# A graph layer's fused kernel: the vectors g and u by VectorE's row sums, u by way of device memory, and the queues ordered anew

## The reference

```python
h = relu(layernorm(x))
q, k, v = h @ Wq + bq, h @ Wk + bk, h @ Wv + bv
adj = zeros(N, N).at[src, dst].set(1)
a = q @ k.T / sqrt(512);  a = a*adj + (1 - adj)*(-1e6)
x = x + softmax(a) @ v
h = relu(layernorm(x))
agg = segment_sum(h[src], dst) / max(deg, 1)
x = x + (h + alpha * (agg @ W.T + b))
```

## Time and profile before

| | |
|---|---|
| median of 3 runs | 240.35 us (240.06 to 240.42) |
| the profiled execution, its own time | 240.38 us |
| its span, first to last instruction | 238.6 us |
| TensorE busy | 232.7 us (98%), 1296 instructions |
| VectorE busy | 163.4 us (68%), 282 |
| ScalarE busy | 80.8 us (34%), 147 |
| GpSimd busy | 71.5 us (30%), 104 |
| granted clock of TensorE | 1.00 in all 40 slices |
| chain that ended last | TensorE 86%, VectorE 10%, DMA 2% |

### The profile page before, as it was taken

The page is one execution under the profiler, slowest core; times in us unless marked ns, Lnnn a source line. Parts: engine busy times, 40 slices in busy tenths (PEclk is TensorE's granted clock), DMA queues, the critical chain, the costliest instruction groups (busy, mean ns, idle before and its releaser), DMA issues.

```text
span 238.6 us, 3313 instructions
## 1 busy us (share of the span) xinstructions
PE 232.7 (98%) x1296; PEld 188.5 (79%) x1296; DVE 163.4 (68%) x282; ACT 80.8 (34%) x147; POOL 71.5 (30%) x104
## 2 busy tenths in 40 slices
PE   7999799999999999999999999999999999999995
PEld 5476489788888888888888888888888888888885
DVE  6999999998979482885749975757574263064222
ACT  3299972843222132233260623232342002060000
POOL 4187172000000019971431643434153306000000
PEclk9999999999999999999999999999999999999999
DMA  6990000000000001040000000000000000001232
GB/s 210 332 371 17 1 3 0 0 3 0 0 3 26 18 3 47 3 140 36 0 0 3 0 0 0 3 0 1 0 0 3 0 0 0 3 3 44 94 122 92
DMA packets 5616, 9.41 MB, mean 39 GB/s; under 512 B 864, under 2 KB 1376, under 8 KB 5600
## 3 DMA queue, kind: packets, MB, share of 16 engines
q1 hardware_dynamic: 4880, 8.91, 10.5%
q10 hardware_dynamic: 720, 0.28, 0.4%
HBM read 7.09 MB, written 2.10 MB: 39 GB/s over the span
## 4 chain that ended last, share of the span: by engine, by line
PE 86%; DVE 10%; DMA 2%; issue 0%; ACTq 0%; DVEq 0%
PE bank L804 22%; PE bank L806 21%; PE bank L805 21%; PE bank L953 12%; PE bank L825 5%; DVE ohW L553 3%; DVE ohL L549 3%; PE bank L973 3%; DMA src_i<-in_src 2%; DVE hT_lo L604 1%; DVE M_lo L634 1%; PE bank L864 1%; PE bank L889 0%; PE bank L851 0%; DVE key_b L540 0%
## 5 line engine op out<-in xcount | busy, mean ns | idle before, releaser
L804 PE MATMUL bank<-V_hi,pT_hi 128*128 128x512 f32 x64 | 25.6, 401 | 0.0
L422 ACT ACTIVATE h2f<-xs,nmr,rstd 128x512 f32<-128x512 f32 x8 | 6.5, 816 | 56.3 <-POOL nmr L365 56.3
L549 DVE TENSOR_TENSOR ohL<-iotaL,lo_b 128x1024 bf16<-128x1024 bf16 x33 | 22.6, 686 | 4.0 <-PE bank L825 4.0
L553 DVE TENSOR_TENSOR ohW<-iotaW,key_b 128x1280 bf16<-128x1280 bf16 (+4 forms) x33 | 25.2, 763 | 0.0
L804 PE MATMUL bank<-hT_hi,GT_hi 128*128 128x512 f32 x64 | 25.1, 392 | 0.0
L806 PE MATMUL bank<-V_hi,pT_lo 128*128 128x512 f32 x64 | 25.0, 391 | 0.0
L806 PE MATMUL bank<-hT_hi,GT_lo 128*128 128x512 f32 x64 | 25.0, 390 | 0.0
L953 PE MATMUL bank<-A,h_hi 128*128 128x512 f32 x64 | 24.9, 389 | 0.0
L953 PE MATMUL bank<-A,h_lo 128*128 128x512 f32 x64 | 24.9, 389 | 0.0
L805 PE MATMUL bank<-hT_lo,GT_hi 128*128 128x512 f32 x64 | 24.9, 389 | 0.0
L805 PE MATMUL bank<-V_lo,pT_hi 128*128 128x512 f32 x64 | 24.9, 389 | 0.0
(11 more groups left out here) (135 smaller groups left out, 528.2 us busy)
## 6 DMA issues: line engine op xcount, KB each, us to landing
xs<-in_x SPq DMA_DIRECT2D x4, 512.0 KB, 9.2
out_dram<-o_sb SPq DMA_DIRECT2D x7, 256.0 KB, 2.0
wq_raw<-in_wqT SPq DMA_DIRECT2D x4, 256.0 KB, 6.4
wk_raw<-in_wkT SPq DMA_DIRECT2D x4, 256.0 KB, 7.1
wv_raw<-in_wv SPq DMA_DIRECT2D x1, 1024.0 KB, 12.7
wt_raw<-in_wT SPq DMA_DIRECT2D x1, 1024.0 KB, 5.4
bv_sb<-in_bv SPq DMA_DIRECT2D x1, 256.0 KB, 3.3
b_sb<-in_b SPq DMA_DIRECT2D x1, 256.0 KB, 3.1
```

The lines of the kernel that those rows point to most:

```text
L422: nc.scalar.activation(out, xs[:, t, :], ACT.Relu, bias=nmr[:, layer, t:t + 1], scale=rstd[:, layer, t:t + 1]).then_inc(relu, 1)
L549: nc.vector.tensor_tensor(ohL[:, q % RING, :, :].rearrange("p b (m two) -> p b m two", two=2), bcast(iotaL[:, :].rearrange("p (m two) -> p ...
L553: nc.vector.tensor_tensor(ohW[:, q % RING, :, 0:row].rearrange("p b (m two) -> p b m two", two=2), bcast(iotaW[:, 0:row].rearrange("p (m t ...
L804: mm(out, lhs[0][a], rhs[0][b], start=(first and k == 0), stop=False)
```

## The change

g and u are no longer summed over partitions by TensorE. wk and wq are loaded a second time, untransposed (`wk_rows`, `wq_rows`, 1 MB each), with bq and bk broadcast to all partitions (256 KB each). VectorE makes each element of g and u by one row sum (four `tensor_tensor_reduce` for each vector, each waiting for the one before). g then stands where it is needed. u stands as four numbers on each partition; SyncE stores it to a line of 2 KB in device memory, waits, and reads it back broadcast to `u_sb`. Steps `g` and `u` of TensorE, VectorE and ScalarE are gone, and there are 20 in place of 21 steps in the rotation of banks. The three orders are written anew and GpSimd has one of its own. The keys are made in fewer VectorE instructions (window numbers are moved by one; the check for edges outside their window becomes two sums on ScalarE, for which `bb` has one more product), the copy `lo_b` goes to ScalarE and the products of biases to GpSimd. The first tile of wk and src change queues. The core of the diff:

```diff
-PE_ORDER = ("Mk0 Mk1 c1 bb c2 M0 c2 T0 c1 M1 T1 c1 T2 c1 M2 c1 M3 c1 T3 c2 G0 T4 G1 G2 g c2 T5 c1 G3 T6 T7 u c3 G4 G5 G6 c3 "
-           "V0 c3 V1 V2 V3 c2 G7 V4 c2 V5 c2 V6 V7 c3")
-ACT_ORDER = ("sum0 sum1 sq0 sum2 sum3 k0 sq1 sq2 rows0 k1 sum4 T0 rows1 sq3 rows2 sum5 T1 T2 k2 sum6 sq4 M0 M1 rows3 M2 M3 "
-           "k3 T3 k4 wv0 rows4 sq5 sum7 sq6 T4 rows5 sq7 k5 G0 T5 rows6 k6 G1 rows7 T6 T7 G2 G3 u G4 k7 wv1 k8 G5 G6 k9 V0 "
-           "k10 V1 V2 k11 V3 G7 k12 k13 V4 V5 V6 k14 V7 k15")
-DVE_ORDER = ("o4 bb o4 T0 o3 T1 T2 M0 o1 M1 M2 M3 T3 gsum o1 usum o2 T4 g wv0 o2 G0 T5 o1 T6 G1 T7 G2 o2 dot0 dot1 G3 dot2 "
-           "wv1 u o2 G4 o2 dot3 G5 dot4 G6 V0 o1 V1 o3 dot5 o1 V2 dot6 V3 G7 o2 V4 dot7 o2 V5 V6 V7")
+PE_ORDER = ("Mk0 Mk1 c3 bb M0 c2 M1 c2 T0 M2 T1 M3 T2 T3 c3 G0 G1 G2 G3 c1 V0 T4 c3 V1 T5 c3 T6 V2 V3 T7 c3 V4 V5 c3 G4 G5 "
+           "G6 c3 V6 c2 G7 c2 V7 c3")
+ACT_ORDER = ("sum0 sum1 sq0 sum2 sq1 sq2 k0 sum3 rows0 M0 k1 sum4 M1 rows1 sq3 T0 rows2 M2 T1 rows3 k2 M3 T2 T3 wv0 k3 wv1 "
+           "sum5 sq4 G0 sq5 rows4 G1 k4 sum6 G2 T4 sq6 rows5 k5 sum7 G3 rows6 k6 T5 sq7 V0 k7 V1 rows7 T6 k8 V2 T7 V3 k9 "
+           "k10 V4 V5 G4 G5 G6 k11 V6 k12 G7 k13 k14 V7 k15")
+DVE_ORDER = ("o7 bb o2 M0 o1 M1 T0 T1 M2 M3 T2 T3 o1 wv0 usum gsum wv1 o1 G0 o2 dot0 G1 dot1 o3 dot2 T4 G2 o1 G3 V0 o1 T5 o1 "
+           "dot3 o1 V1 dot4 o1 T6 o1 V2 T7 V3 dot5 V4 o1 V5 o1 dot6 dot7 o1 G4 G5 G6 o2 V6 o4 G7 o1 V7")
+POOL_ORDER = ("sum0 sum1 sum2 sq0 sq1 sum3 sq2 sum4 sq3 sum5 sq4 sq5 sum6 sq6 sum7 sq7")
...
-        g_terms = place("g_terms", [P, 2, D], F32, r_G + 16 * KB)
-        u_terms = place("u_terms", [P, 2, D], F32, r_V + 24 * KB)
-        t_g, t_u = g_terms[:, 1, :], u_terms[:, 1, :]
+        wk_rows = place("wk_rows", [P, KD, D], F32, r_V + 16 * KB)
+        wq_rows = place("wq_rows", [P, KD, D], F32, r_V + 24 * KB)
+        bq_row, g_scr = (place(n, [P, D], F32, r_G + (16 + 2 * i) * KB) for i, n in enumerate(("bq_row", "g_scr")))
...
+        bk_row = place("bk_row", [P, D], F32, r_R + 6 * KB)
...
-                for raw, w_d, loaded in ((wq_raw, wqT_d, ld_wq), (wk_raw, wkT_d, ld_wk)):
-                    sp.dma_start(raw[:, k, :], w_d[k * P:(k + 1) * P, :]).then_inc(loaded[k], 16)
+                sp.dma_start(wq_raw[:, k, :], wqT_d[k * P:(k + 1) * P, :]).then_inc(ld_wq[k], 16)
+                if k == 0:
+                    sp.dma_start(src_i[:, :], src_d).then_inc(ld_edges, 16)
+                else:
+                    sp.dma_start(wk_raw[:, k, :], wkT_d[k * P:(k + 1) * P, :]).then_inc(ld_wk[k], 16)
             rows_in(2)
             rows_in(3)
             sp.dma_start(wv_raw[:, :, :], wv_d.rearrange("(k p) n -> p k n", p=P)).then_inc(ld_wv, 16)
+            sp.dma_start(wk_rows[:, :, :], wk_d.rearrange("(k p) n -> p k n", p=P)).then_inc(ld_g, 16)
+            sp.dma_start(bq_row[:, :], bqrow_d.partition_broadcast(P)).then_inc(ld_g, 16)
+            sp.wait_ge(strays, 2)
+            sp.dma_start(wq_rows[:, :, :], wq_d.rearrange("(p k) n -> p k n", k=KD)).then_inc(ld_u, 16)
+            sp.dma_start(bk_row[:, :], bkrow_d.partition_broadcast(P)).then_inc(ld_u, 16)
+            sp.wait_ge(u_dots, KD)
+            sp.dma_start(u_d.rearrange("(p k) -> p k", k=KD), u_col[:, :]).then_inc(u_out, 16)
+            sp.wait_ge(u_out, 16)
+            sp.dma_start(u_sb[:, :], u_d.partition_broadcast(P)).then_inc(u_back, 16)
...
-            for step, n in ACT_STEPS:
+            pool.wait_ge(ld_bqk, 32)
+            link(nc.gpsimd.tensor_scalar(bqk_s[:, :, :], bqk[:, :, :], SCALE, None, ALU.mult))
+            nc.gpsimd.tensor_tensor(bprod[:, 0:KD], bqk_s[:, 0, :], bqk[:, 1, :], ALU.mult).then_inc(vec_ready, 1)
+            for step, n in POOL_STEPS:
...
+            act.dma_start(wk_raw[:, 0, :], wkT_d[0:P, :]).then_inc(ld_wk[0], 16)
             act.dma_start(dst_i[:, :], dst_d).then_inc(ld_edges, 16)
-            act.dma_start(src_i[:, :], src_d).then_inc(ld_edges, 16)
...
+            act.wait_ge(src_low, 1)
+            nc.scalar.activation(lo_b[:, :, :], bcast(key_i[0][:, :], 2, 2), ACT.Copy).then_inc(tables, 1)
+            act.wait_ge(past, 1)
+            nc.scalar.activation(stray[:, 0, :], key_t[0][:, :], ACT.Relu, bias=1.0, scale=-1.0,
+                                 accum_out=bprod[:, KD:KD + 1]).then_inc(strays, 1)
+            nc.scalar.activation(stray[:, 1, :], key_t[2][:, :], ACT.Relu,
+                                 accum_out=bprod[:, KD + 1:KD + 2]).then_inc(strays, 1)
...
                 dve.wait_ge(ld_edges, 32)
-                nc.vector.tensor_scalar(key_i[0][:, :], src_i[:, :], P - 1, None, ALU.bitwise_and)
+                nc.vector.tensor_scalar(key_i[0][:, :], src_i[:, :], P - 1, None, ALU.bitwise_and).then_inc(src_low, 1)
                 nc.vector.tensor_scalar(key_i[1][:, :], src_i[:, :], N - P, None, ALU.bitwise_and)
                 link(nc.vector.tensor_tensor(key_t[0][:, :], dst_i[:, :], win0[:, :], ALU.subtract))
-                nc.vector.tensor_copy(lo_b[:, :, :], bcast(key_i[0][:, :], 2, 2))
-                nc.vector.scalar_tensor_tensor(out=key_t[1][:, :], in0=key_i[1][:, :], scalar=1.0 / P, in1=wide[:, :],
-                                               op0=ALU.mult, op1=ALU.mult)
-                link(nc.vector.tensor_tensor(key_t[2][:, :], key_t[0][:, :], wide[:, :], ALU.is_lt))
-                link(nc.vector.scalar_tensor_tensor(out=key_t[3][:, :], in0=key_t[0][:, :], scalar=0.0,
-                                                    in1=key_t[2][:, :], op0=ALU.is_ge, op1=ALU.mult))
-                link(nc.vector.scalar_tensor_tensor(out=key_t[1][:, :], in0=key_t[1][:, :], scalar=1.0, in1=key_t[0][:, :],
-                                                    op0=ALU.add, op1=ALU.add))
-                link(nc.vector.tensor_tensor(key_b[:, :, :], bcast(key_t[1][:, :], 2, 2), bcast(key_t[3][:, :], 2, 2), ALU.mult))
-                nc.vector.tensor_reduce(bprod[:, KD:KD + 1], key_t[3][:, :], AX.X, ALU.min)
-                dve.wait_ge(tables, 2)
+                link(nc.vector.scalar_tensor_tensor(out=key_t[1][:, :], in0=key_i[1][:, :], scalar=1.0 / P, in1=wide[:, :],
+                                                    op0=ALU.mult, op1=ALU.mult))
+                nc.vector.tensor_tensor(key_b[:, :, :], bcast(key_t[1][:, :], 2, 2), bcast(key_t[0][:, :], 2, 2), ALU.add)
+                nc.vector.tensor_tensor(key_t[2][:, :], key_t[0][:, :], wide[:, :], ALU.subtract).then_inc(past, 1)
+                dve.wait_ge(tables, 3)
+                dve.wait_ge(past, 1)
...
-            dve.wait_ge(ld_bqk, 32)
-            link(nc.vector.tensor_scalar(bqk_s[:, :, :], bqk[:, :, :], SCALE, None, ALU.mult))
-            nc.vector.tensor_tensor(bprod[:, 0:KD], bqk_s[:, 0, :], bqk[:, 1, :], ALU.mult).then_inc(vec_ready, 1)
...
-                elif step in ("gsum", "usum"):
-                    weights, raw, terms, done = (0, wk_raw, g_terms, g_sum) if step == "gsum" else (1, wq_raw, u_terms, u_sum)
-                    for k in range(KD):
-                        dve.wait_ge((ld_wk if step == "gsum" else ld_wq)[k], 16)
-                    link(nc.vector.tensor_scalar(terms[:, 0, :], raw[:, 0, :], bqk_s[:, weights, 0:1], None, ALU.mult))
-                    for k in range(1, KD):
-                        ins = nc.vector.scalar_tensor_tensor(
-                            out=terms[:, k % 2, :], in0=raw[:, k, :], scalar=bqk_s[:, weights, k:k + 1],
-                            in1=terms[:, (k - 1) % 2, :], op0=ALU.mult, op1=ALU.add)
-                        if k < KD - 1:
-                            link(ins)
-                    ins.then_inc(done, 1)
+                elif step == "gsum":
+
+                    dve.wait_ge(ld_g, 32)
+                    for m in range(KD):
+                        if m:
+                            dve.wait_ge(g_dots, m)
+                        nc.vector.tensor_tensor_reduce(
+                            out=g_scr[:, :], in0=wk_rows[:, m, :], in1=bq_row[:, :], scale=SCALE, scalar=0.0, op0=ALU.mult,
+                            op1=ALU.add, accum_out=g0[:, m:m + 1]).then_inc(g_kept if m == KD - 1 else g_dots, 1)
+                elif step == "usum":
+
+                    dve.wait_ge(ld_u, 32)
+                    for m in range(KD):
+                        if m:
+                            dve.wait_ge(u_dots, m)
+                        nc.vector.tensor_tensor_reduce(
+                            out=uh[0][:, :], in0=wq_rows[:, m, :], in1=bk_row[:, :], scale=SCALE, scalar=0.0, op0=ALU.mult,
+                            op1=ALU.add, accum_out=u_col[:, m:m + 1]).then_inc(u_dots, 1)
...
-                elif step == "g":
-                    dve.wait_ge(g_ps, 1)
-                    nc.vector.tensor_copy(g0[:, :], bank[7][:, 0:KD]).then_inc(g_kept, 1)
-                elif step == "u":
-                    i = proj_index((step, n))
-                    dve.wait_ge(proj_hi, i + 1)
-
```

(17 more changed lines are left out.)

43 lines of the change are left out of this document (25 added, 18 removed).

## The result

The changed kernel takes 236.27 us, the median of five runs (235.85 to 236.94); the kernel before 240.35 us. The ratio is 0.983, with a 95% interval of 0.982 to 0.985: 4.1 us or 1.7% faster. The profiled execution took 236.27 us for a span of 234.5.

A forecast was written before the change was run, and what follows sets the result against it. TensorE was taken to set the time, with VectorE and ScalarE as full early on. Terms -0.45 - 1.35 + 0.1 - 1.65 + 0.2 = -3.15 us took 240.38 to 237.2 us, range 236.6 to 239.0.

The forecast's parts named there:

- (1): First loads: wk's first tile goes out earlier, removing TensorE's wait for it, -0.45 us (bounds -0.48 to 0).
- (2): TensorE up to G0: 10 batches instead of 12 ahead of it, G0 at 26.55, wait cut by 1.35 us.
- (2) k0: ScalarE's copy of group 0's counts, needed by batch 3: a TensorE wait of 0.1 us.
- (3): Products of g and u leave TensorE with nothing in their place: -1.65 us, called sure without a new wait.
- (4): g and u as eight VectorE row sums, 0.73 us each, hidden with 0.1 to 0.2 us spare: cost 0 (bounds 0, +1.0).
- (A): VectorE becomes the bound between 26 and 49 us, costing 1.0 to 1.2 us: 238.3 us, chance 0.14.
- (5): u's trip through device memory before dot0: 6.0 us under 8.8 us of cover, no cost.
- (C): Reordering gives nothing as ScalarE holds G0; only the removed products count: 238.9 us, chance 0.11.

The follow-up runs named there:

- p3_late_batch: Kernel before with the twelfth batch of edges moved behind T3's low half on VectorE and behind T4 on TensorE: 240.42 us, ratio 0.9999.
- p5_no_gu_no_sums: Kernel before without TensorE's g and u products and without VectorE's sums for them, g and u holding other values: 239.46 us, ratio 0.996.
- p1_no_gu: Kernel before without TensorE's g and u products, copies of VectorE's terms standing in, VectorE's sums kept: 240.35 us, ratio 0.9996.
- a1_orders_alone: Changed kernel with g and u made as before, keeping the new orders, keys and first loads: 238.25 us, ratio 0.991 to the kernel before.
- a4_four_more: Changed kernel with four more chained, unread row sums on VectorE after gsum: 239.35 us, ratio 0.996 to the kernel before.
- a2_longer_keys: Changed kernel with four more linked 264-column instructions on VectorE ahead of the first one-hots: 236.52 us, ratio 0.984 to the kernel before.
- a5_first_loads_back: Changed kernel with the first loads (wk's first tile, src) on their queues as before: 236.78 us, ratio 0.984 to the kernel before.

## Why the prediction was right, and where it wasn't

**Its measure of the gain.** Forecast 3.15 us, measured 4.11. The accounts of both, by TensorE's timeline (minus is a gain):

| step | forecast | measured |
|---|---|---|
| (1) first product of wk and wq starts earlier | -0.45 | -0.43 |
| the 16 products to the first batch | 0 | +0.47 |
| (2) the wait before G0, with what is left of it | -1.35 | -1.70 + 0.15 |
| waits inside records: the last pair before G0, T6 and T7 | 0 | -0.27 - 0.27 |
| (2) k0 | +0.1 | 0 |
| (2) one more product in bb | +0.2 | +0.21 |
| (3) products of g and u | -1.65 | -1.66 |
| the rest, most of it in short waits inside records | 0 | -0.37 |
| from the scores to the end | 0 | -0.24 |
| sum | -3.15 | -4.11 |

**The step that failed is (2), in its term for the pair of batches ahead of G0.** The forecast took the pair at its record, 1.65 us, moved it along as work and kept its cost. A pair elsewhere in the same trace takes 1.20 from start to start:

```profile
39.38 1.36 PE L825 MATMUL bank<-ohW,ohL 128*128 128x160 bf16 x21
40.58 0.60 PE L864 MATMUL bank<-ident,h 128*128 128x128 f32 x4
```

The other 0.45 us were waiting. Of these 0.27 lie inside the pair: its second product had to wait until ScalarE had copied a finished group of columns out of its bank (a `k` step). ScalarE's copy and TensorE's weight loads, in the kernel before:

```profile
26.34 0.59 ACT L450 ACTIVATE A<-bank 128x512 fp32r<-128x512 f32 x1
...
26.99 1.12 PEld L825 LDWEIGHTS bank<-ohW,ohL 128*128 128x128 bf16 x20 [0.34 <-ACT A L450]
```

The copy ends at 26.93. The next one-hots, which VectorE writes from 26.50 to 27.32, are ready when TensorE comes to them, at 27.50; and in p3_late_batch, where the twelfth batch is gone from there, the same wait of 0.34 us of the weight loads for the copy is still seen. The other 0.18 us are the tail of the last record. Records of products of edges are 0.23 us long, but the next one starts after 0.07, so up to 0.16 us of waiting behind one shows as no idle time. G0 starts 1.74 us after the last product of the pair and 0.03 would do: its wait was 1.70 us and not the 1.50 of the earlier trace rows.

In the changed kernel both are gone but for 0.15 us. So is 0.27 us of the same kind in T6 and T7 (1.16 to 0.87 us from start to start), where T7 waited for VectorE's low half of T5. These are the largest part of the miss. The slower products at the start (+0.47) hid some of it; counted from the first batch, where they don't enter, the forecast's scores come 1.2 us too late. Of the other parts 0.37 us lies in many small steps, among them waits in the kernel before of 0.22 us at T0 for its rows, 0.10 for one-hots and 0.08 at G4. TensorE's 334 products of edges take 20.42 us from start to start before and 18.28 after, and waits account for the whole difference. The last 0.24 us lie behind the scores, where the code is the same; what makes that piece isn't settled (150.6 us in before, p3_late_batch and p5_no_gu_no_sums, about 150.4 in most others).

**Step (3) had the right sum for a wrong reason, which is luck.** The text says "sure" of 1.65 us. In the kernel before the products were worth nothing (p1_no_gu), since VectorE held G4; in the new orders they are worth 1.88 (a1_orders_alone). The opening reading, that TensorE sets the time with two waits to win, misses that up to 48 us VectorE set it. The forecast saw VectorE at 16.30 of 16.30 us and drew the risk for the changed kernel from it, but not the question for the present one: whether TensorE's seemingly unbroken work there was being let go step by step. The 1.5 us before G0, too, would not have been a gain alone (p3_late_batch). The parts are not additive: products 0, moved batch 0, products and sums both gone 0.9 to 1.1, orders with keys and loads 2.1, all 4.1.

**Step (1).** The first product did start 0.43 us earlier, and TensorE's wait for wk is gone, but the 16 products to the first batch took 7.41 instead of 6.94 us, for the reason told below; in the run shown nothing was left. The first one-hots start at 7.54, forecast 7.6.

```profile
5.04 0.30 DVE L554 TENSOR_SCALAR key_i<-src_i 128x264 int32<-128x264 int32 x1 [0.46 <-DMA src_i<-in_src]
...
7.54 0.69 DVE L569 TENSOR_TENSOR ohL<-iotaL,lo_b 128x1024 bf16<-128x1024 bf16 x1
```

The edges didn't come later behind the 256 KB tiles: VectorE's keys start at 5.04, where they started at 5.17. From issue to landing dst took 3.4 us (before: 3.3) and src 3.8 (3.9). dst, issued 0.4 us later behind the tile of wk, did land later, but src is the last of the two in both kernels. The Trainium skill's alternation of each engine between its queues (DMA: Bandwidth & Descriptors, section Queues, rings and completion order), by which the forecast allowed for a delay up to 0.5 us, cost nothing here.

**Step (2), the rest.** G0 at 26.75 where 26.55 was forecast and 26.4 to 26.7 given. Counted from the first batch it is 14.78 against 15.07 forecast. It starts 0.78 us after T3's low half again, and 0.18 us after the last product of edges, where 0.03 would do: 0.15 us of wait that no row of TensorE shows.

**Step (4) was right, the 0.73 us to the hundredth.** VectorE's timeline: two of the eight row sums, G0's low half, dot0.

```profile
29.04 0.68 DVE L616 CUSTOM_DVE_ANT_0 uh<-wq_rows,bk_row 128x512 f32<-128x512 f32 x1
...
29.77 0.69 DVE L616 CUSTOM_DVE_ANT_0 uh<-wq_rows,bk_row 128x512 f32<-128x512 f32 x1
...
37.15 0.74 DVE L653 SCALAR_TENSOR_TENSOR GT_lo<-bank,g,GT_hi 128x512 fp32r<-128x512 f32 x1
...
40.48 0.68 DVE L636 CUSTOM_DVE_ANT_0 uh<-h,u_sb 128x512 f32<-128x512 f32 x1
```

0.73 us from one row sum to the next, as worked out from the dots and the 0.12 us of a link. gsum ends at 34.7, G0's low half at 37.8 (forecast 38.0), V0 starts at 38.32 (38.2), V2 at 48.87 (48.7), with no wait. Rival (A) didn't come, by the 0.33 us that a4_four_more measured.

**Step (5) was right.** SyncE's issues and the two transfers' entries among the DMA issues (KB, us to landing):

```profile
31.96 0.33 SPq L325 DMA_DIRECT2D u_dram<-u_col  x1
34.63 0.33 SPq L327 DMA_DIRECT2D u_sb<-u_dram  x1
```

```profile
u_sb<-u_dram SPq DMA_DIRECT2D x1, 256.0 KB, 3.1
...
u_dram<-u_col SPq DMA_DIRECT2D x1, 2.0 KB, 2.6
```

From 31.96 to 34.63 + 3.1 = 37.7 us is 5.7 us, both issues included, where the forecast had 6.0; dot0 starts at 40.48 without a wait, 2.8 us later. The store of 2 KB took 2.6 us in this execution and 2.0 to 2.1 in those of the seven other kernels that have it. That agrees with the Trainium skill's fixed cost of about 2 us (DMA: Bandwidth & Descriptors, section Anatomy of one DMA), though the section has it for transfers that GpSimd issues and these are SyncE's; the long delays that it warns of didn't show here.

**Rival (C)** gave the reordering nothing. With keys and loads, which a2_longer_keys and a5_first_loads_back price at 0.3 and 0 us, it gave 2.1 us, and without it the products are worth nothing: the rival had the two parts the wrong way round. ScalarE did hold TensorE, but by the 0.27 us told above.

**The range** was too narrow at its low end, because all bounds there were for terms that the waits view had named. A bound for what records hide would have been 0.7 us more.

## What to carry to other kernels

Where two engines are both full, hold their timelines side by side and look for steps that start a constant time (here 0.78 us) after the other engine's instruction: they are let go by it, though their own row shows no wait. Compare the same step at several places from start to start; the one that is longer hides a wait, and the waits of the weight loads with a narrow window name what ended it. A line of the waits over the whole span doesn't say where its waits lie. And price an edit on the engine that looks like the bound only together with the edit that lets it go: in the old order the removed products gave 0, the moved batch 0, products and sums together about 1 us, while the whole change gave 4.1.
